# Feed-forward blocks: the input's two transposed halves and the sum of squares in one group of transposes, with the ring of banks used in another order

## The chip, the cores and the metric

The kernel runs on one core of one Trainium2 chip. The metric is the device time of one execution in microseconds (us). Three runs of the kernel before gave 552.25, 552.31 and 552.56 us.

## The reference

The input x has 8 sequences of 1024 tokens with 256 channels. First comes a linear attention with 16 heads (softmax over the head's columns for q, over the tokens for k, a 16 x 16 state for each head), a layer norm, an output projection, the residual and a layer norm. Then comes the feed-forward part, which is what the change touches:

```python
h = layer_norm(x, ln1_g, ln1_b)
h = jnp.einsum('bsd,hd->bsh', h, ternary_quant(w1)) + b1
h = jax.nn.gelu(h, approximate=False)
h = layer_norm(h, ln2_g, ln2_b)
out = jnp.einsum('bsh,dh->bsd', h, ternary_quant(w2)) + b2
...
x = _layernorm(x + _L0_ffn_ref(x, ...), axis=-1)
```

The hidden width is 1024; w1 and w2 are rounded to three values. Everything is float32.

## The kernel before, in words

Every engine has its own hand-written order of work, and semaphores tie the orders together. The attention of the eight sequences fills roughly the first half of the time. The feed-forward part follows, in 16 blocks k of 512 tokens (TB = 4 tiles of 128), and its first three blocks are interleaved with the end of the attention. The names below are the functions of the code; F, S and T are short forms used in this text.

For one block k:

- `ff_norm_apply` (VectorE) scales the four token tiles. `ff_transposes(k, c)` (TensorE, L1945; **T0** and **T1** for c = 0, 1) transposes one half of the channels of the four tiles into one bank, with four 128 x 128 transposes. `ff_ht_high(k, c)` (ScalarE, L854) writes the high part of the bank, `ff_ht_low(k, c)` (VectorE, L1359) the rest.
- `ff_first(k, m)` (TensorE, L2005, **F0** to **F7**) makes 128 of the 1024 hidden columns for 512 tokens with four matmuls. `ff_gelu(k, m)` (ScalarE, L863) works in place in the bank. `ff_square_and_high(k, m)` (ScalarE) writes the square (L879) and the high part (L881). `ff_act_low(k, m)` (VectorE, L1367) writes the rest, `ff_a_lo`.
- `ff_second(k, m)` (TensorE, L2027, **S0** to **S7**) adds both parts times w2 into the four banks of y, with two matmuls for each of four token tiles t. S0 overwrites the banks, and so waits for `ff_centre_y` of the block before, once for each tile t.
- The hidden layer norm is applied after the second product. `ff_hidden_mean` (VectorE, L1391) reads a sum that the second product leaves beside y; `ff_centre_y` (VectorE, L1398, one instruction for each tile) subtracts mean times a row. The squares are summed over the hidden columns on GpSimd (L588) and VectorE (L1378, L1385), and `ff_sum_transposes(k)` (TensorE, L1960) transposes the sum, which `ff_hidden_stats` (VectorE, L1406) reduces.
- `ff_residual`, `ff_out_stats`, `ff_out_shift` (VectorE), `ff_out_rstd` (GpSimd) and `ff_normalise_out` (ScalarE, L896) make the output, `ff_store` (SyncE) writes it.

**The ring.** Banks 0 to 3 are a ring. A block uses 11 places: eight for F, two for T, one for the sum. The place of each use, modulo 4, is its bank (`FIRST_AT`, `HT_AT`, `SUM_AT`), and TensorE waits before each use for what was read last from that bank: `ff_bank_free(k, m)` waits for both the high and the low part of F(k, m). The places follow the order in which TensorE works.

**The order on TensorE** in block k (the loop in the tensor block): T1(k+1), sum(k-1), F3, F4, S0, F5, F6, S1, S2, F7, F0(k+1), S3, F1(k+1), S4, S5, T0(k+2), F2(k+1), S6, S7. So four transposes stand between S5 and F2, and eight between S7 and F3.

**The order on ScalarE** around it: square and high of m = 0 and 1, high part of T0, gelu, square and high of m = 2, two tiles of the output's normalisation, high part of T1, two tiles more, gelu of m = 3 and 4. **On VectorE**: low parts of m = 0 and 1, low part of T0, hidden mean, low part of m = 2, centring of tiles 0 to 3, low part of T1, hidden statistics.

In blocks 1 and 2 ScalarE still has work of the attention between these: `squares` (L812) and `normalise` (L820), four instructions each.

Of the kernel before, what the change touches and what calls it, by code (L numbers as in the profile page):

```python
# [58 lines left out]
def both_halves(nc, x_tok, x_first, x_chan, wq, wk, wv, wo, w1, w2, vecs_d, rows_d, ident_d, mask_d, x1_scratch, out):  # L59
# [3 lines left out]
    CH = C // P  # L63
# [15 lines left out]
    FIRST_AT = (9, 10, 12, 15, 16, 17, 18, 19)  # L79
    HT_AT = (0, 2)  # L80
# [10 lines left out]
    with ExitStack() as ctx:  # L91
# [604 lines left out]
        def _(act):  # L696
# [118 lines left out]
            def normalise(b, g):  # L815
# [3 lines left out]
                for t in range(g * GROUP, (g + 1) * GROUP):  # L819
# [237 lines left out]
            ff_ht_high(2, 0)  # L1057
            ff_gelu(1, 2)
            ff_square_and_high(1, 2)
            squares(NB - 1, 1)  # L1060
            ff_ht_high(2, 1)
# [15 lines left out]
            ff_ht_high(3, 0)  # L1077
            ff_gelu(2, 2)
            ff_square_and_high(2, 2)
            normalise(NB - 2, 0)  # L1080
            ff_ht_high(3, 1)
            ff_gelu(2, 3)
            ff_gelu(2, 4)
            for k in range(3, NK):
# [12 lines left out]
                ff_ht_high(k + 1, 0)  # L1097
                ff_gelu(k, 2)
                ff_square_and_high(k, 2)
                ff_normalise_out(k - 3, (0, 1))  # L1100
# [38 lines left out]
        def _(dve):  # L1139
# [507 lines left out]
            ff_act_low(1, 1)  # L1647
            ff_ht_low(2, 0)
            ff_hidden_mean(0)
            ff_act_low(1, 2)  # L1650
            ff_centre_y(0, (0, 1))
            ff_centre_y(0, (2, 3))
            ff_ht_low(2, 1)
            ff_hidden_stats(0)
            for k in range(1, NK - 1):
# [17 lines left out]
                ff_act_low(k + 1, 1)  # L1673
                ff_ht_low(k + 2, 0)
                ff_hidden_mean(k)
                ff_act_low(k + 1, 2)
                ff_centre_y(k, (0, 1))
                ff_centre_y(k, (2, 3))
                ff_ht_low(k + 2, 1)
                ff_hidden_stats(k)  # L1680
# [31 lines left out]
        def _(pe):  # L1712
# [215 lines left out]
            def ff_transposes(k, c):  # L1928
# [3 lines left out]
                if k == 0 and c == 0:  # L1932
                    pe.wait_ge(et_lo_ok, PAIRS * (NB - 1) + 1)
                if k == 0 and c == 1:
                    pe.wait_ge(et_lo_ok, PAIRS * (NB - 1) + 3)
                if k == 1 and c == 0:
                    pe.wait_ge(et_lo_ok, PAIRS * (NB - 1) + 4)
                if c == 0:
                    if k >= 2:
                        ff_bank_free(k - 2, 6)  # L1940
# [23 lines left out]
            def ff_first(k, m):  # L1964
# [12 lines left out]
                elif m == 2:  # L1977
                    if k < 1:
                        pe.wait_ge(ff_ht_lo_ok, CH * k + 1)
                    else:  # L1980
                        ff_bank_free(k - 1, 7)
                elif m == 3:
                    if k < NK - 1:
                        pe.wait_ge(ff_ht_lo_ok, CH * (k + 1) + 1)
                    else:
                        ff_bank_free(k - 1, 6)
                elif m == 4:
                    ff_bank_free(k, 2)
# [12 lines left out]
                if k == 0 and m == 0:  # L2001
                    pe.wait_ge(et_lo_ok, PAIRS * (NB - 1) + 2)
# [146 lines left out]
            ff_transposes(2, 0)  # L2149
# [82 lines left out]
```

## Time and profile before

| | us |
|---|---|
| median of 3 runs | 552.31 (552.25 to 552.56) |
| the profiled execution | 551.79 |
| its span, first to last instruction | 549.9 |
| TensorE matmul busy | 532.1 (97%) |
| VectorE busy | 481.8 (88%) |
| ScalarE busy | 478.6 (87%) |
| GpSimd busy | 414.7 (75%) |

A busy time is the union of an engine's instructions. Matmuls are pipelined: one matmul's recorded time overlaps the next, and what a matmul costs is the distance from its start to the next one's start (its pitch). The same holds for ScalarE and VectorE, where an instruction's recorded end lies up to 0.1 us behind the start of the next. The idle time in square brackets is that of the engine before the row, with what ended it.

### The profile page before, as it was taken

What the parts mean: (1) busy time and instruction counts of PE and PEld (TensorE: products, weight loads), DVE (VectorE), ACT (ScalarE), POOL (GpSimd) and SP (SyncE); (2) the same over time, 40 slices, a digit from 0 to 9 for tenths busy, and PEclk for the clock granted to TensorE, in tenths of its full rate; (3) what the DMA queues carried; (4) which work ended last, traced back from release to release, by engine and by line L of the source; (5) the groups of instructions that cost most, each with busy time, mean ns of one, the idle gap of its engine ahead of it and who ended that gap; (6) DMA issues with size and microseconds to landing.
All of it is one profiled execution on the core that took longest, in us unless ns stands there. A gap on an engine that the chain in (4) does not pass through costs nothing.

```text
span 549.9 us, 10913 instructions
## 1 busy us (share of the span) xinstructions
PE 532.1 (97%) x3541; PEld 492.0 (89%) x3541; DVE 481.8 (88%) x1227; ACT 478.6 (87%) x952; POOL 414.7 (75%) x429
## 2 busy tenths in 40 slices
PE   8999999999999999989999999999999999999993
PEld 7999999898999989879987999999999999999992
DVE  5888998989899898878788899999999999999896
ACT  5745789798978878778799999999999999999996
POOL 2965969877796986478468878888888877776782
PEclk9999999999999999999999999999999999999997
DMA  8530050320705021070011003322125253010012
GB/s 337 203 122 1 1 230 2 131 100 11 297 1 229 2 87 69 1 266 5 0 40 41 1 0 117 117 76 79 50 68 116 78 93 94 34 53 38 39 40 114
DMA packets 12679, 46.51 MB, mean 85 GB/s; under 512 B 1360, under 2 KB 3792, under 8 KB 10448
## 3 DMA queue, kind: packets, MB, share of 16 engines
q1 hardware_dynamic: 12336, 45.28, 23.7%
q8 instruction: 29, 0.48, 0.4%
q10 hardware_dynamic: 288, 0.54, 0.3%
q14 instruction: 26, 0.21, 0.1%
HBM read 29.01 MB, written 16.81 MB: 83 GB/s over the span
## 4 chain that ended last, share of the span: by engine, by line
PE 68%; ACT 11%; DVE 11%; POOL 5%; issue 3%; DMA 2%; SPq 0%; POOLq 0%; DVEq 0%; ACTq 0%
PE ring L2005 19%; PE qps_sps_aps_then_y L2027 19%; PE qps_sps_aps_then_y L1787 5%; PE qps_sps_aps_then_y L1893 5%; PE qps_sps_aps_then_y L1873 5%; PE ring L1815 5%; DVE z L1285 3%; PE ring L1945 2%; POOL xt_lo L462 2%; PE ring L1920 1%; PE ring L1908 1%; PE ring L1960 1%; ACT ek L745 1%; DMA xc<-in_x_first_dram 1%; POOL ff_accp_over_xt_lo L588 1%
## 5 line engine op out<-in xcount | busy, mean ns | idle before, releaser
L2027 PE MATMUL qps_sps_aps_then_y<-ff_w_over_xc_lo,ff_a_lo_over_qw 128*128 128x258 f32 x512 | 126.5, 283 | 0.0
L2027 PE MATMUL qps_sps_aps_then_y<-ff_w_over_xc_lo,ff_a_hi_over_xc_lo 128*128 128x258 f32 x512 | 126.4, 283 | 0.0
L1367 DVE SCALAR_TENSOR_TENSOR ff_a_lo_over_qw<-ring,ff_rho,ff_a_hi_over_xc_lo 128x512 fp32r<-128x512 f32 x128 | 92.8, 743 | 12.5 <-ACT ff_a_hi_over_xc_lo L881 11.4
L2005 PE MATMUL ring<-ff_ht_hi_over_qw,t 128*128 128x512 f32 x256 | 103.7, 405 | 0.1
L2005 PE MATMUL ring<-ff_ht_lo_over_xc_hi,t 128*128 128x512 f32 x256 | 100.5, 393 | 0.0
L2027 PEld LDWEIGHTS qps_sps_aps_then_y<-ff_w_over_xc_lo,ff_a_lo_over_qw 128*128 128x128 f32 x512 | 96.8, 189 | 3.3
L2027 PEld LDWEIGHTS qps_sps_aps_then_y<-ff_w_over_xc_lo,ff_a_hi_over_xc_lo 128*128 128x128 f32 x512 | 96.7, 189 | 3.4
L863 ACT ACTIVATE ring<-ring,bias 128x512 f32<-128x512 f32 x128 | 84.5, 689 | 6.7 <-PE ring L2005 5.5
L588 POOL TENSOR_TENSOR ff_accp_over_xt_lo<-ff_accp_over_xt_lo,ff_sq_over_ek_et_hi 128x512 f32<-128x512 f32 x66 | 86.0, 1303 | 2.0
L879 ACT ACTIVATE ff_sq_over_ek_et_hi<-ring 128x512 f32<-128x512 f32 x128 | 80.5, 629 | 0.5
L881 ACT CAST ff_a_hi_over_xc_lo<-ring 128x512 fp32r<-128x512 f32 x128 | 79.5, 621 | 0.0
L2005 PEld LDWEIGHTS ring<-ff_ht_hi_over_qw,t 128*128 128x128 f32 x256 | 48.2, 188 | 8.8 <-issue 0.9
L575 POOL TENSOR_TENSOR ff_x1c_over_xt_hi<-ff_x_over_w_raw_xc,ff_c_row 128x512 f32<-128x512 f32 x32 | 37.5, 1192 | 23.9 <-DVE ff_z_over_et_lo L1427 23.9
L2005 PEld LDWEIGHTS ring<-ff_ht_lo_over_xc_hi,t 128*128 128x128 f32 x256 | 48.2, 188 | 7.3
L483 POOL TENSOR_TENSOR qw<-qw,qinv 128x1024 f32<-128x1024 f32 x16 | 31.1, 1942 | 22.2 <-DVE qinv L1186 22.0
L1873 PE MATMUL qps_sps_aps_then_y<-r_hi,pt_hi 128*128 128x384 f32 x128 | 44.7, 349 | 0.7 <-DVE r_lo L1144 0.7
L1873 PE MATMUL qps_sps_aps_then_y<-r_lo,pt_hi 128*128 128x384 f32 x128 | 43.2, 337 | 0.0
L1873 PE MATMUL qps_sps_aps_then_y<-r_hi,pt_lo 128*128 128x384 f32 x128 | 43.1, 337 | 0.0
L462 POOL TENSOR_TENSOR xt_lo<-xt,xt_hi 128x1024 fp32r<-128x1024 f32 x16 | 38.5, 2407 | 2.0 <-ACT xt_hi L728 0.8
L1296 DVE BATCH_NORM_STATS2 bnA<-qps_sps_aps_then_y 128x6 f32<-128x256 f32 x64 | 27.3, 426 | 14.1 <-PE qps_sps_aps_then_y L1873 14.0
L1893 PE MATMUL qps_sps_aps_then_y<-et_hi,xt_hi 128*128 128x256 f32 x128 | 37.4, 292 | 1.9 <-ACT z L776 1.8
L473 POOL TENSOR_TENSOR xt<-xt,c_row 128x1024 f32<-128x1024 f32 x16 | 38.6, 2414 | 0.7
(200 smaller groups left out, 1615.4 us busy)
## 6 DMA issues: line engine op xcount, KB each, us to landing
xt<-in_x_tok_dram SPq DMA_DIRECT2D x8, 1024.0 KB, 4.8
out_dram<-ff_z_over_et_lo SPq DMA_DIRECT2D x15, 512.0 KB, 2.7
x_scratch<-z SPq DMA_DIRECT2D x14, 514.0 KB, 3.6
ff_x_over_w_raw_xc<-x_scratch SPq DMA_DIRECT2D x14, 514.0 KB, 5.1
xc<-in_x_chan_dram SPq DMA_DIRECT2D x6, 1024.0 KB, 6.9
w_raw<-in_w_dram SPq DMA_DIRECT2D x2, 1024.0 KB, 5.4
ek<-in_x_chan_dram SPq DMA_DIRECT2D x1, 1024.0 KB, 8.2
x_scratch<-xt SPq DMA_DIRECT2D x2, 512.0 KB, 7.9
```

What stands on the lines that cost most here:

```text
L462: nc.gpsimd.tensor_tensor(xt_lo[:, ts], xt[:, b % 2, ts], xt_hi[:, ts].bitcast(F32), ALU.subtract).then_inc(xt_lo_ok, 1)
L473: nc.gpsimd.tensor_tensor(xt[:, b % 2, ts], xt[:, b % 2, ts], c_row[:].rearrange("p (o c) -> p o c", o=1).to_broadcast([P, GROUP, C]), ALU ...
L575: nc.gpsimd.tensor_tensor(ff_x1c[:, k % 2, ts], ff_x1[:, k % XB, ts, 0:C], ff_c_row[:].rearrange("p (o c) -> p o c", o=1).to_broadcast([P, ...
L588: nc.gpsimd.tensor_tensor(ff_accp[:], a, ff_sq[:, m], ALU.add).then_inc(ff_sum_p, 1)
L863: nc.scalar.activation(ff_bank(k, m), ff_bank(k, m), ACT.Gelu, bias=bias1[:, m:m + 1]).then_inc(ff_gelu_ok, 1)
L879: nc.scalar.activation(ff_sq[:, m], ff_bank(k, m), ACT.Square).then_inc(ff_sq_ok, 1)
L881: nc.scalar.copy(ff_a_hi[:, m % DEPTH], ff_bank(k, m)).then_inc(ff_hi_ok, 1)
L1367: nc.vector.scalar_tensor_tensor(out=ff_a_lo[:, m % DEPTH], in0=ff_bank(k, m), scalar=ff_rho[:, m:m + 1], in1=ff_a_hi[:, m % DEPTH].bitcas ...
L1873: last = nc.tensor.matmul(out, l, r, start=(c == 0 and k == 0), stop=(c == CH - 1 and k == 2), skip_group_check=True)
L1893: last = nc.tensor.matmul(sps[:, a * C:(a + 1) * C], x, e, start=(t == 0 and a == 0 and k == 0), stop=(t == T - 1 and k == 2), skip_group_ ...
L2005: mm = nc.tensor.matmul(ff_bank(k, m), t1[:, c, m * P:(m + 1) * P], h[:, k % 2, c], start=(c == 0 and j == 0), stop=(c == CH - 1 and j == 1))
L2027: last = nc.tensor.matmul(ff_yps[:, t, 0:C + 2], a[:, m % DEPTH, t * P:(t + 1) * P], ff_w2[:, m], start=(m == 0 and j == 0), stop=(m == FC ...
```

## The change

T0 moves from between S5 and F2 to the place just before T1, so that T0(k+1), T1(k+1) and sum(k-1) stand together, twelve transposes in a row between S7 and F3. The ring's places are changed to this order (`FIRST_AT[2]` from 12 to 11, `HT_AT` from (0, 2) to (1, 2)), and with them the waits: F3 now waits for both parts of F2 of its own block, F4 for the low part of T0, F2 for F6 of the block before. The orders on ScalarE and VectorE are changed to match: on ScalarE one tile of the output's normalisation stands where the high part of T0 stood, and both high parts follow each other; in block 1 `squares` comes after both high parts. On VectorE the low part of m = 2 comes before the hidden mean, and the low parts of T0 and T1 stand between the centring of tile 0 and that of tiles 1 to 3. In block 2 the four `normalise` tiles are split 1, 1 and 2.

```diff
@@ -76,8 +76,8 @@
     TOK = TB * P
     NK = NB * T // TB
     RING = 4
-    FIRST_AT = (9, 10, 12, 15, 16, 17, 18, 19)
-    HT_AT = (0, 2)
+    FIRST_AT = (9, 10, 11, 15, 16, 17, 18, 19)
+    HT_AT = (1, 2)
     SUM_AT = 25
     USES = FC + CH + 1
     DEPTH = 4
@@ -812,11 +812,11 @@
                     nc.scalar.activation(zjunk[:, t % GROUP], z_tile(b, t), ACT.Square, bias=znm[:, t:t + 1],
                                          accum_out=zss[:, t:t + 1]).then_inc(z_sq, 1)
 
-            def normalise(b, g):
+            def normalise(b, g, tiles=range(GROUP)):
                 if not 0 <= b < NB:
                     return
                 act.wait_ge(z_fin, 4 * (NG * b + g + 1))
-                for t in range(g * GROUP, (g + 1) * GROUP):
+                for t in (g * GROUP + n for n in tiles):
                     nc.scalar.activation(z_tile(b, t), z_tile(b, t), ACT.Identity, bias=nmr[:, b % RZ, t:t + 1],
                                          scale=rsZ[:, b % RZ, t:t + 1]).then_inc(x1_ok, 1)
 
@@ -1054,11 +1054,11 @@
             ff_gelu(1, 1)
             ff_square_and_high(1, 0)
             ff_square_and_high(1, 1)
-            ff_ht_high(2, 0)
             ff_gelu(1, 2)
             ff_square_and_high(1, 2)
+            ff_ht_high(2, 0)
+            ff_ht_high(2, 1)
             squares(NB - 1, 1)
-            ff_ht_high(2, 1)
             normalise(NB - 3, 1)
             ff_gelu(1, 3)
             ff_gelu(1, 4)
@@ -1074,11 +1074,13 @@
             ff_gelu(2, 1)
             ff_square_and_high(2, 0)
             ff_square_and_high(2, 1)
-            ff_ht_high(3, 0)
+            normalise(NB - 2, 0, (0,))
             ff_gelu(2, 2)
             ff_square_and_high(2, 2)
-            normalise(NB - 2, 0)
+            normalise(NB - 2, 0, (1,))
+            ff_ht_high(3, 0)
             ff_ht_high(3, 1)
+            normalise(NB - 2, 0, (2, 3))
             ff_gelu(2, 3)
             ff_gelu(2, 4)
             for k in range(3, NK):
@@ -1094,10 +1096,11 @@
                 ff_gelu(k, 1)
                 ff_square_and_high(k, 0)
                 ff_square_and_high(k, 1)
-                ff_ht_high(k + 1, 0)
+                ff_normalise_out(k - 3, (0,))
                 ff_gelu(k, 2)
                 ff_square_and_high(k, 2)
-                ff_normalise_out(k - 3, (0, 1))
+                ff_normalise_out(k - 3, (1,))
+                ff_ht_high(k + 1, 0)
                 ff_ht_high(k + 1, 1)
                 ff_normalise_out(k - 3, (2, 3))
                 ff_gelu(k, 3)
@@ -1645,12 +1648,12 @@
             ff_square_total(0)
             ff_act_low(1, 0)
             ff_act_low(1, 1)
+            ff_act_low(1, 2)
+            ff_hidden_mean(0)
+            ff_centre_y(0, (0,))
             ff_ht_low(2, 0)
-            ff_hidden_mean(0)
-            ff_act_low(1, 2)
-            ff_centre_y(0, (0, 1))
-            ff_centre_y(0, (2, 3))
             ff_ht_low(2, 1)
+            ff_centre_y(0, (1, 2, 3))
             ff_hidden_stats(0)
             for k in range(1, NK - 1):
                 ff_norm_apply(k + 2, (0, 1))
@@ -1671,12 +1674,12 @@
                 ff_residual(k - 1, (2, 3))
                 ff_act_low(k + 1, 0)
                 ff_act_low(k + 1, 1)
+                ff_act_low(k + 1, 2)
+                ff_hidden_mean(k)
+                ff_centre_y(k, (0,))
                 ff_ht_low(k + 2, 0)
-                ff_hidden_mean(k)
-                ff_act_low(k + 1, 2)
-                ff_centre_y(k, (0, 1))
-                ff_centre_y(k, (2, 3))
                 ff_ht_low(k + 2, 1)
+                ff_centre_y(k, (1, 2, 3))
                 ff_hidden_stats(k)
             ff_out_stats(NK - 3, (2, 3))
             ff_act_low(NK - 1, 3)
@@ -1930,14 +1933,14 @@
                     return
                 pe.wait_ge(ff_n_ok, TB * (k + 1))
                 if k == 0 and c == 0:
-                    pe.wait_ge(et_lo_ok, PAIRS * (NB - 1) + 1)
+                    pe.wait_ge(et_lo_ok, PAIRS * (NB - 1) + 2)
                 if k == 0 and c == 1:
                     pe.wait_ge(et_lo_ok, PAIRS * (NB - 1) + 3)
                 if k == 1 and c == 0:
-                    pe.wait_ge(et_lo_ok, PAIRS * (NB - 1) + 4)
+                    pe.wait_ge(et_lo_ok, PAIRS * (NB - 1) + 1)
                 if c == 0:
                     if k >= 2:
-                        ff_bank_free(k - 2, 6)
+                        ff_bank_free(k - 2, 7)
                 else:
                     if k >= 1:
                         ff_bank_free(k - 1, 0)
@@ -1976,16 +1979,16 @@
                         ff_bank_free(k - 1, 5)
                 elif m == 2:
                     if k < 1:
-                        pe.wait_ge(ff_ht_lo_ok, CH * k + 1)
+                        pe.wait_ge(et_lo_ok, PAIRS * NB)
                     else:
-                        ff_bank_free(k - 1, 7)
+                        ff_bank_free(k - 1, 6)
                 elif m == 3:
+                    ff_bank_free(k, 2)
+                elif m == 4:
                     if k < NK - 1:
                         pe.wait_ge(ff_ht_lo_ok, CH * (k + 1) + 1)
                     else:
-                        ff_bank_free(k - 1, 6)
-                elif m == 4:
-                    ff_bank_free(k, 2)
+                        ff_bank_free(k - 1, 7)
                 elif m == 5:
                     if k < NK - 1:
                         pe.wait_ge(ff_ht_lo_ok, CH * (k + 1) + 2)
@@ -1998,8 +2001,6 @@
                         pe.wait_ge(ff_r_sum, k)
                 elif m == 7:
                     ff_bank_free(k, 3)
-                if k == 0 and m == 0:
-                    pe.wait_ge(et_lo_ok, PAIRS * (NB - 1) + 2)
                 for c in range(CH):
                     for j, h in enumerate((ff_ht_hi, ff_ht_lo)):
                         mm = nc.tensor.matmul(ff_bank(k, m), t1[:, c, m * P:(m + 1) * P], h[:, k % 2, c],
@@ -2146,11 +2147,11 @@
             ff_first(1, 1)
             ff_second(0, 4)
             ff_second(0, 5)
-            ff_transposes(2, 0)
             ff_first(1, 2)
             ff_second(0, 6)
             ff_second(0, 7)
             for k in range(1, NK + 1):
+                ff_transposes(k + 1, 0)
                 ff_transposes(k + 1, 1)
                 ff_sum_transposes(k - 1)
                 ff_first(k, 3)
@@ -2166,7 +2167,6 @@
                 ff_first(k + 1, 1)
                 ff_second(k, 4)
                 ff_second(k, 5)
-                ff_transposes(k + 2, 0)
                 ff_first(k + 1, 2)
                 ff_second(k, 6)
                 ff_second(k, 7)
```

## Rows read from the trace of the kernel before

**Rows 1.** The page: busy time and share of TensorE, and its granted clock in 40 slices.

```profile
PE 532.1 (97%) x3541; PEld 492.0 (89%) x3541; DVE 481.8 (88%) x1227; ACT 478.6 (87%) x952; POOL 414.7 (75%) x429
...
PEclk9999999999999999999999999999999999999997
```

**Rows 2.** Twelve blocks: busy PE, PEld, DVE, ACT, POOL, then the granted clock.

```profile
312.97:509.61 196.64, 196.64 (x1298) 180.26 (x1297) 183.20 (x457) 190.73 (x362) 155.77 (x156) 1.00 0.24 71
```

**Rows 3.** Timeline of TensorE around a block's transposes: start us, length us, what.

```profile
391.62 0.60 PE L1945 MATMUL ring<-ident,ff_xn 128*128 128x128 f32 x4
...
392.29 0.39 PE L2005 MATMUL ring<-ff_ht_lo_over_xc_hi,t 128*128 128x512 f32 x1
...
394.91 0.60 PE L1945 MATMUL ring<-ident,ff_xn 128*128 128x128 f32 x4
...
396.01 0.40 PE L2005 MATMUL ring<-ff_ht_lo_over_xc_hi,t 128*128 128x512 f32 x1
...
397.63 0.28 PE L2027 MATMUL qps_sps_aps_then_y<-ff_w_over_xc_lo,ff_a_hi_over_xc_lo 128*128 128x258 f32 x1
...
398.35 0.28 PE L2027 MATMUL qps_sps_aps_then_y<-ff_w_over_xc_lo,ff_a_hi_over_xc_lo 128*128 128x258 f32 x1
```

**Rows 4.** Timeline of ScalarE, the same stretch.

```profile
391.91 0.61 ACT L881 CAST ff_a_hi_over_xc_lo<-ring 128x512 fp32r<-128x512 f32 x1
...
393.19 0.66 ACT L863 ACTIVATE ring<-ring,bias 128x512 f32<-128x512 f32 x1
393.89 0.60 ACT L879 ACTIVATE ff_sq_over_ek_et_hi<-ring 128x512 f32<-128x512 f32 x1
394.38 0.58 ACT L881 CAST ff_a_hi_over_xc_lo<-ring 128x512 fp32r<-128x512 f32 x1
394.85 1.10 ACT L896 ACTIVATE ff_z_over_et_lo<-ff_z_over_et_lo,ff_nmr,ff_rsZ 128x256 f32<-128x256 f32 x2
395.84 0.69 ACT L854 ACTIVATE ff_ht_hi_over_qw<-ring,ff_gain 128x512 fp32r<-128x512 f32 x1
396.41 1.09 ACT L896 ACTIVATE ff_z_over_et_lo<-ff_z_over_et_lo,ff_nmr,ff_rsZ 128x256 f32<-128x256 f32 x2
```

**Rows 5.** Timeline of VectorE, the same stretch.

```profile
395.11 0.17 DVE L1391 TENSOR_REDUCE ff_nmu<-qps_sps_aps_then_y 128x4 f32<-128x8 f32 x1 [0.56 <-PE qps_sps_aps_then_y L2027]
395.31 0.75 DVE L1367 SCALAR_TENSOR_TENSOR ff_a_lo_over_qw<-ring,ff_rho,ff_a_hi_over_xc_lo 128x512 fp32r<-128x512 f32 x1
395.98 1.65 DVE L1398 SCALAR_TENSOR_TENSOR ff_yc_over_xt_lo<-ff_u_row,ff_nmu,qps_sps_aps_then_y 128x256 f32<-128x256 f32 x4
397.54 0.75 DVE L1359 SCALAR_TENSOR_TENSOR ff_ht_lo_over_xc_hi<-ring,ff_gain,ff_ht_hi_over_qw 128x512 fp32r<-128x512 f32 x1
398.20 0.68 DVE L1406 TENSOR_REDUCE ff_sums<-ring 128x4 f32<-128x512 f32 x1
```

**Rows 6.** Timeline of TensorE and VectorE in block 1.

```profile
295.81 0.63 PE L1945 MATMUL ring<-ident,ff_xn 128*128 128x128 f32 x4 [0.94 <-DVE ff_a_lo_over_qw L1367]
...
300.12 0.51 PE L2005 MATMUL ring<-ff_ht_hi_over_qw,t 128*128 128x512 f32 x1
300.46 0.40 PE L2005 MATMUL ring<-ff_ht_lo_over_xc_hi,t 128*128 128x512 f32 x1
...
299.32 0.74 DVE L1359 SCALAR_TENSOR_TENSOR ff_ht_lo_over_xc_hi<-ring,ff_gain,ff_ht_hi_over_qw 128x512 fp32r<-128x512 f32 x1
```

**Rows 7.** Timeline of ScalarE in blocks 1 and 2.

```profile
295.30 0.52 ACT L812 ACTIVATE zjunk<-xt,znm 128x256 f32<-128x256 f32 x1
...
297.28 0.67 ACT L854 ACTIVATE ff_ht_hi_over_qw<-ring,ff_gain 128x512 fp32r<-128x512 f32 x1
...
299.82 1.21 ACT L863 ACTIVATE ring<-ring,bias 128x512 f32<-128x512 f32 x2
...
310.47 0.87 ACT L854 ACTIVATE ff_ht_hi_over_qw<-ring,ff_gain 128x512 fp32r<-128x512 f32 x1
```

**Rows 8.** Waits of TensorE over the whole span: total us, times, longest us.

```profile
PE ring L1960 <- POOL ff_accp_over_xt_lo L588: 0.6, 1, 0.6
```

## The prediction, made before the changed kernel ran

> **What bounds the kernel now.** I read the page first: TensorE is busy for 97% of the span and its granted clock is full in every slice but the last [rows 1]. Then the busy times over twelve whole blocks: TensorE is busy in 196.64 of 196.64 us, so a block takes 16.39 us and TensorE never waits; ScalarE has 190.73 us of work in them and VectorE 183.20 [rows 2], which leaves them 0.49 and 1.12 us a block. The feed-forward part is bound by TensorE's stream, and the change can gain only by taking something out of it, or lose by making it wait. So the rest is a walk along one block, in the timelines of TensorE, ScalarE and VectorE [rows 3 to 5], all in the clock of one block (its T1 at 394.91). The last views are the start-up [rows 6, 7] and the one wait near the end [rows 8].
>
> **The change, part by part.** No instruction is added or removed, and no DMA is moved; SyncE's and GpSimd's orders stay.
>
> *One group instead of two.* T0 alone costs 0.44 us: it starts at 391.62, F2's second matmul at 392.29, less the first matmul's own 0.23 (seven such matmuls lie between 396.01 and S0's start at 397.63) [rows 3]. T1 and the sum together cost 396.01 - 0.23 - 394.91 = 0.87 us [rows 3]. Eight transposes cost twice what four cost, so entering or leaving such a group is free, and a group of twelve will cost 1.31. I take a gain of 0.01 us a block, within the two decimals of the rows. From above it is bound by one transpose, 0.11.
>
> *F2 earlier by 0.44, T0 later.* F2 starts at 391.62, S6 and S7 end 0.44 earlier, T0 starts at 394.47, T1 stays at 394.91, the sum and F3 stay. F2 waits for F6 now, which was read one place earlier than F7: no cost. T0 waits for F7 of two blocks before, long read.
>
> *F3 waits for F2's parts.* ScalarE's new order, with the pitches of rows 4: high part of m = 1 at 391.91; one tile of normalisation at 392.38 (+0.47, as from 394.38 to 394.85); gelu of m = 2 at 392.88 (+0.50, half of 394.85 to 395.84; its bank is ready at 393.19 - 0.44 = 392.75, so ScalarE's queue decides); square +0.70 = 393.58; high part +0.49 = 394.07, which ends 0.58 later, 394.65. ScalarE to VectorE takes 0.03 (gelu's end at 393.85 to the square at 393.89 is of that size) [rows 4]. VectorE is idle by then (it was idle for 0.56 before 395.11 [rows 5]), so the low part of m = 2 runs from 394.68 to 395.43. F3 should start at 396.01 - 0.23 = 395.78: met, with 0.18 to spare after the 0.17 hop found below. No stall.
>
> *The chain behind it.* This is where I expect the loss. From 394.68 VectorE does, by rows 5: low part of m = 2 (0.67, from 395.31 to 395.98), mean (0.20), centring of tile 0 (0.39, a quarter of 395.98 to 397.54), low part of T0 (0.66), low part of T1 (0.66), and centring of tiles 1, 2, 3. These start at 395.35, 395.55, 395.94, 396.60, 397.26, 397.65 and 398.04; the last ends 0.48 later, at 398.52. High parts of T0 and T1 are no limit: T0's bank is ready near 395.1, so they end near 395.8 and 396.4. The hop from VectorE to a waiting matmul is 0.17: in block 1 the low part ends at 299.32 + 0.74 = 300.06, and F5 really runs from 300.46 - 0.23 = 300.23 [rows 6]. So the low part of T0, ended at 396.69, lets F4 go at 396.86 where it was due at 396.71: 0.15 late. S0's fourth tile, due at 398.35 [rows 3], can go at 398.69: 0.34 late, the first stall included. Before, all four tiles were centred by 397.63, when S0 began. Net of the 0.01 it is **0.33 us a block**. It does not heal: gelu of m = 2 hangs on ScalarE's queue, which starts behind F1, and between F1 and S0 TensorE has no slack to shift. It recurs in blocks 3 to 14: 12 x 0.33 = 4.0 us. Bounds: a hop of 0.03 everywhere makes it 0.20 less, so 0.14; were tile 0's transposed low parts slowed as 0.1 us of contention, 0.43. I take 0.33, from rows that show each instruction in this very place.
>
> What hides the rest: the hidden statistics start 0.23 later (398.43 for 398.20), and F6, which waits for them, starts only 1.3 us behind; GpSimd's wait for them grows by as much and it has 3.4 us a block to spare [rows 2].
>
> *Start-up.* In block 1 T1 waits 0.94 us for a low part and is over at 296.44 [rows 6]. Before, `squares` filled this time on ScalarE from 295.30 to 297.28, and the high part of T1 came after [rows 7]. Now the high part comes first and cannot start before 296.48; `squares` follow at 297.05, end 1.98 later, `normalise` takes 1.97 (299.82 - 297.28 - 0.57), and gelu of m = 3 starts at 301.00 instead of 299.82: 1.18 late. From there ScalarE has no idle time up to 310.47 [rows 7], so all of it arrives in block 2: tile of `normalise` at 311.65, gelu 312.15, square 312.85, high part 313.34 to 313.92, and by the same chain (0.03, 3.36 to the last centring, 0.48, 0.17) S0's fourth tile at 317.96. It was due 3.44 behind T1, at 394.91 - 5 x 16.39 + 3.44 = 316.40. So blocks 1 and 2 together lose **1.56 us**. Bounds: 0.6 if ScalarE's delay is caught up, 1.8.
>
> *The end.* Block 15 has no T, only the sum, so F3 stands 0.88 nearer to F2 and waits some 0.7 us. The last sum of squares hides it: TensorE waits 0.6 us there for GpSimd [rows 8], whose additions do not hang on these matmuls closely. I count 0 to 0.2, and take 0.
>
> **Sum.** 4.0 + 1.56 = 5.5 us on the profiled execution's 551.79, so 557.3. That execution is 0.52 below the median of the runs, so I expect **557.8 us**.
>
> *A rule weighed against the rows.* The hops are 0.03 from engine to engine and 0.17 to a matmul in rows 4 and 6. The Trainium skill, Advanced Engine Details and Errata, section Miscellaneous Facts, has 50 to 100 ns for a sequencer's read of a semaphore. With 0.1 at both ScalarE hops the block would lose 0.14 more, some 2 us in all; the rows decide, and they say 0.03.
>
> **The rivals.**
>
> *No wait, same time.* F3's and S0's waits are all met, because VectorE's chain is 0.34 us shorter than I add up. For it: TensorE waits nowhere in twelve blocks now [rows 2], and VectorE has 1.12 us a block free. Against it: the chain starts at ScalarE, not at VectorE's free time, and each length is read in place. It decides at one point: the third centring of the three must end by 398.18. With start-up lag hidden too: 552.2. Chance 0.13.
>
> *The seam was dear.* Each group costs a fixed time beside its transposes, and one is saved. The most the rows leave is 0.11 a block, over 14 blocks 1.5 us: 550.8. Against it: 0.44 and 0.87 [rows 3]. Chance 0.03.
>
> *Only the steady loss.* ScalarE catches up its 1.18 us before block 2: 13 x 0.33 = 4.3, so 556.6. Chance 0.18, slower too.
>
> *The chain is longer.* ScalarE and VectorE slow each other down on the banks, 0.5 us a block: 12 x 0.5 + 1.8, so 560.1. Chance 0.08.
>
> *The clock falls.* Twelve transposes in a row lower TensorE's granted clock, and the eight-matmul stretch behind each group runs at 1.2 instead of 2.4 GHz: 14 x 8 x 0.23 = 26 us, so 578. Against it: the clock stays full through groups of four and of eight, behind TensorE's full work [rows 1, 2]. Chance 0.02. The Trainium skill, TensorE: Matmul & The Clock Gate, Part 4, says that transposes do not count as busy for the gate; by that rule a longer group could cost this.
>
> That the group is not one group can be left out: T1 and the sum wait for the parts of m = 0 and 1, which both engines make before those of m = 2, and these are there in time for F3.
>
> **How the numbers follow.** My forecast has 0.56, the two other slower ones near it 0.26, the clock 0.02: slower 0.84. No wait 0.13: same. Seam 0.03, and 0.01 of the case without waits: faster 0.04, same 0.12. Two runs of this kernel can be told apart from 0.2% on, 1.1 us. The range leaves out the cases without a loss (0.16) and the clock: it begins at 553.8, with both bounds low (12 x 0.14 and nothing from start-up would be 554.0), and ends at 560.2, the longer chain.
>
> **What would show it.** In the changed profile: twelve transposes cost 1.31 us; TensorE idle, or a longer pitch, before F4 and inside S0 at its third and fourth tile, released by VectorE L1398; a period near 16.7 us; in block 1 an idle ScalarE before the second L854, and gelu of m = 3 over 1 us later. I am wrong if the period is still 16.39, or if the waits stand at F3.

## The result, and the profile after

| | before | after |
|---|---|---|
| median, us | 552.28 (551.65 to 552.56, 4 runs) | 559.73 (559.60 to 560.07, 4 runs) |
| the profiled execution, its span | 551.79, 549.9 | 559.60, 557.6 |
| ratio | | 1.0136 (95% interval 1.0124 to 1.0148) |

The changed kernel is slower by 7.45 us; 5.5 were forecast. One execution of block0_place, below, took 750.67 us at a mean granted clock of 0.66, and no number here counts it. In the changed kernel lines have moved by 1 (F is L2006, S L2028) or by 3: T is L1948, the sum L1963, the low parts L1370 and L1362, mean L1394, centring L1401. First the page, which answers to [rows 1], and the busy times over eleven whole blocks, which answer to [rows 2] (PE, PEld, DVE, ACT, POOL, then the granted clock).

```profile
PE 538.4 (97%) x3541; PEld 492.4 (88%) x3541; DVE 483.9 (87%) x1227; ACT 481.3 (86%) x952; POOL 414.5 (74%) x429
...
PEclk9999999999999999999999999999999999999998
```

```profile
331.40:515.80 184.40, 184.40 (x1191) 165.35 (x1190) 169.39 (x418) 176.24 (x331) 141.49 (x144) 1.00 0.27 75
```

TensorE is still shown busy without a gap and at the full clock, for the same 3541 matmuls, and yet a block takes 184.40 / 11 = 16.76 us where it took 16.39. The busy share hides the loss. In the block below a matmul that has waited is recorded as 0.39 or 0.50 us long, where 0.28 or 0.39 is normal, and its record still overlaps that of the matmul before, so no gap appears. Only the starts show the wait. One block in the timeline of TensorE, which answers to [rows 3]:

```profile
398.47 1.04 PE L1948 MATMUL ring<-ident,ff_xn 128*128 128x128 f32 x8
399.34 0.60 PE L1963 MATMUL ring<-ident,ff_accd_over_xt_lo 128*128 128x128 f32 x4
399.70 0.48 PE L2006 MATMUL ring<-ff_ht_hi_over_qw,t 128*128 128x512 f32 x1
400.02 0.40 PE L2006 MATMUL ring<-ff_ht_lo_over_xc_hi,t 128*128 128x512 f32 x1
...
400.77 0.50 PE L2006 MATMUL ring<-ff_ht_hi_over_qw,t 128*128 128x512 f32 x1
401.11 0.40 PE L2006 MATMUL ring<-ff_ht_lo_over_xc_hi,t 128*128 128x512 f32 x1
...
401.81 0.28 PE L2028 MATMUL qps_sps_aps_then_y<-ff_w_over_xc_lo,ff_a_hi_over_xc_lo 128*128 128x258 f32 x1
...
402.60 0.39 PE L2028 MATMUL qps_sps_aps_then_y<-ff_w_over_xc_lo,ff_a_hi_over_xc_lo 128*128 128x258 f32 x1
402.82 0.28 PE L2028 MATMUL qps_sps_aps_then_y<-ff_w_over_xc_lo,ff_a_lo_over_qw 128*128 128x258 f32 x1
402.94 0.40 PE L2006 MATMUL ring<-ff_ht_hi_over_qw,t 128*128 128x512 f32 x1
```

The group of twelve costs 400.02 - 0.23 - 398.47 = 1.32 us: nothing is gained at the seam. F3 does not wait (0.32 to its second matmul; the first after transposes starts early in the records and cost the same before). F4's pitch is 0.34 instead of 0.23. In S0 the third tile's two matmuls and the fourth's first have pitches of 0.14, 0.17 and 0.22 where 0.12 is normal. From 401.81 to F5 at 402.94 are 1.13 us, and eight pitches of 0.12 would be 0.96. Now ScalarE, which answers to [rows 4], and VectorE, to [rows 5]:

```profile
396.89 0.69 ACT L863 ACTIVATE ring<-ring,bias 128x512 f32<-128x512 f32 x1
397.61 0.60 ACT L879 ACTIVATE ff_sq_over_ek_et_hi<-ring 128x512 f32<-128x512 f32 x1
398.10 0.58 ACT L881 CAST ff_a_hi_over_xc_lo<-ring 128x512 fp32r<-128x512 f32 x1
398.57 0.61 ACT L896 ACTIVATE ff_z_over_et_lo<-ff_z_over_et_lo,ff_nmr,ff_rsZ 128x256 f32<-128x256 f32 x1
399.11 1.27 ACT L854 ACTIVATE ff_ht_hi_over_qw<-ring,ff_gain 128x512 fp32r<-128x512 f32 x2
```

```profile
398.72 0.75 DVE L1370 SCALAR_TENSOR_TENSOR ff_a_lo_over_qw<-ring,ff_rho,ff_a_hi_over_xc_lo 128x512 fp32r<-128x512 f32 x1 [0.81 <-ACT ff_a_hi_over_xc_lo L881]
399.38 0.15 DVE L1394 TENSOR_REDUCE ff_nmu<-qps_sps_aps_then_y 128x4 f32<-128x8 f32 x1
399.57 0.48 DVE L1401 SCALAR_TENSOR_TENSOR ff_yc_over_xt_lo<-ff_u_row,ff_nmu,qps_sps_aps_then_y 128x256 f32<-128x256 f32 x1
399.97 1.40 DVE L1362 SCALAR_TENSOR_TENSOR ff_ht_lo_over_xc_hi<-ring,ff_gain,ff_ht_hi_over_qw 128x512 fp32r<-128x512 f32 x2
401.29 1.25 DVE L1401 SCALAR_TENSOR_TENSOR ff_yc_over_xt_lo<-ff_u_row,ff_nmu,qps_sps_aps_then_y 128x256 f32<-128x256 f32 x3
```

The chain of the prediction is there link by link: VectorE idles 0.81 us for the high part of m = 2, then low part, mean, centring, two low parts, three centrings, the last of which ends at 402.54. S0's last tile really starts at 402.82 - 0.12 = 402.70. In ten blocks (4 to 13) this hop is 0.16 us each time, and the one from T0's low part to F4 0.16 or 0.17.

**Where the 7.7 us of span go.** The table compares where F0 of a block starts with the kernel before and takes differences, so the attention's own scatter (its first F0 starts 0.35 us earlier to 0.78 later than before, from one kernel to the next) is the first column and no part of the rest. The runs of the next section stand in it as well.

| span compared with before, us | attention | block 0 | blocks 1, 2 | blocks 3 to 14 (per block) | block 15, end | sum |
|---|---|---|---|---|---|---|
| after | -0.05 | 0.91 | 1.63 | 4.51 (0.376) | 0.76 | 7.76 |
| centre_first | 0.35 | 0.90 | 1.42 | 2.33 (0.194) | 0.77 | 5.77 |
| gelu_first | -0.35 | 0.91 | 0.92 | 0.74 (0.061) | 0.59 | 2.80 |
| gelu_first_squares | -0.08 | 0.92 | 0.04 | 0.61 (0.051) | 0.60 | 2.09 |
| own_places | 0.52 | 0.91 | 1.59 | 4.52 (0.377) | 1.13 | 8.67 |
| own_places_2 | 0.53 | 0.89 | 1.60 | 4.44 (0.370) | -0.03 | 7.43 |
| block0_place | 0.07 | -0.15 | 2.10 | 4.43 (0.369) | 0.76 | 7.22 |
| all_terms | 0.49 | -0.14 | 0.53 | 0.69 (0.058) | -0.02 | 1.55 |
| all_terms_total | 0.63 | -0.16 | 0.31 | 0.70 (0.058) | -0.03 | 1.45 |
| before_centre_late | 0.78 | -0.02 | 1.52 | 3.63 (0.302) | 0.02 | 5.93 |
| before_total_late | -0.10 | -0.01 | -0.15 | 0.00 | -0.01 | -0.27 |

Two terms were not in the forecast's sum: F3's waits in block 0 and at the end. Among TensorE's waits over the span:

```profile
PE ring L2006 <- DVE ff_a_lo_over_qw L1370: 1.8, 3, 0.8
...
PE ring L1948 <- DVE ff_a_lo_over_qw L1370: 0.8, 1, 0.8
```

The three waits of the first line are F3's, in blocks 0 (0.83 us), 2 (0.46) and 15 (0.54). The second line is T1's wait in block 1, which was 0.94 before [rows 6]. In block 0, in the timelines of TensorE and VectorE:

```profile
278.43 0.34 PE L1876 MATMUL qps_sps_aps_then_y<-r_lo,pt_hi 128*128 128x384 f32 x1
279.59 0.47 PE L2006 MATMUL ring<-ff_ht_hi_over_qw,t 128*128 128x512 f32 x1 [0.83 <-DVE ff_a_lo_over_qw L1370]
```

```profile
277.71 0.74 DVE L1362 SCALAR_TENSOR_TENSOR ff_ht_lo_over_xc_hi<-ring,ff_gain,ff_ht_hi_over_qw 128x512 fp32r<-128x512 f32 x1
278.37 0.42 DVE L1299 BATCH_NORM_STATS2 bnA<-qps_sps_aps_then_y 128x6 f32<-128x256 f32 x1
278.71 0.74 DVE L1370 SCALAR_TENSOR_TENSOR ff_a_lo_over_qw<-ring,ff_rho,ff_a_hi_over_xc_lo 128x512 fp32r<-128x512 f32 x1
```

F3 of block 0 now waits for the low part of F2, which VectorE makes behind a transposed low part and an attention statistic; it ends at 279.45. Before, F3 did not need it. At the end, F3 of block 15:

```profile
532.56 0.61 PE L1963 MATMUL ring<-ident,ff_accd_over_xt_lo 128*128 128x128 f32 x4
533.70 0.47 PE L2006 MATMUL ring<-ff_ht_hi_over_qw,t 128*128 128x512 f32 x1 [0.54 <-DVE ff_a_lo_over_qw L1370]
```

From the transposes' start to its own are 1.14 us, and in the kernel own_places_2 below, where it does not wait, 0.36. The kernel before's wait for GpSimd [rows 8] is gone, and still all of the delay reaches the last instruction. The timeline of block 1 on ScalarE answers to [rows 7]:

```profile
295.78 0.69 ACT L854 ACTIVATE ff_ht_hi_over_qw<-ring,ff_gain 128x512 fp32r<-128x512 f32 x1
297.23 0.69 ACT L854 ACTIVATE ff_ht_hi_over_qw<-ring,ff_gain 128x512 fp32r<-128x512 f32 x1 [0.77 <-PE ring L1948]
297.82 0.50 ACT L812 ACTIVATE zjunk<-xt,znm 128x256 f32<-128x256 f32 x1
...
301.76 1.21 ACT L863 ACTIVATE ring<-ring,bias 128x512 f32<-128x512 f32 x2
```

ScalarE idles 0.77 us where the squares used to stand, and gelu of m = 3 starts at 301.76 for 299.82.

### The profile page after: what moved, and what is told of

The parts are those of the page before. It is cut to its first block, busy times and chain, and to the rows that moved or that the text cites. A ratio compares the mean times of both kernels' runs of the same rounds, so it can differ in the third digit from the quotient of the medians.

```text
span 557.6 us, 10898 instructions
## 1 busy us (share of the span) xinstructions
PE 538.4 (97%) x3541; PEld 492.4 (88%) x3541; DVE 483.9 (87%) x1227; ACT 481.3 (86%) x952; POOL 414.5 (74%) x429
## 4 chain that ended last, share of the span: by engine, by line
PE 60%; ACT 14%; DVE 12%; POOL 8%; issue 4%; DMA 1%; POOLq 0%; DVEq 0%; ACTq 0%
PE ring L2006 18%; PE qps_sps_aps_then_y L2028 18%; PE qps_sps_aps_then_y L1790 5%; PE qps_sps_aps_then_y L1876 4%; PE qps_sps_aps_then_y L1896 4%; PE ring L1818 4%; DVE z L1288 3%; POOL xt_lo L462 3%; PE ring L1948 2%; POOL xt L473 2%; ACT ff_a_hi_over_xc_lo L881 2%; ACT z L820 1%; ACT ff_sq_over_ek_et_hi L879 1%; POOL xc_lo L452 1%; PE ring L1923 1%
## 5 line engine op out<-in xcount | busy, mean ns | idle before, releaser
L2028 PE MATMUL qps_sps_aps_then_y<-ff_w_over_xc_lo,ff_a_hi_over_xc_lo 128*128 128x258 f32 x512 | 128.7, 286 | 0.0
L2028 PE MATMUL qps_sps_aps_then_y<-ff_w_over_xc_lo,ff_a_lo_over_qw 128*128 128x258 f32 x512 | 127.5, 283 | 0.0
L1370 DVE SCALAR_TENSOR_TENSOR ff_a_lo_over_qw<-ring,ff_rho,ff_a_hi_over_xc_lo 128x512 fp32r<-128x512 f32 x128 | 92.8, 745 | 25.9 <-ACT ff_a_hi_over_xc_lo L881 25.5
L2006 PE MATMUL ring<-ff_ht_hi_over_qw,t 128*128 128x512 f32 x256 | 104.4, 408 | 2.1 <-DVE ff_a_lo_over_qw L1370 1.8
L2028 PEld LDWEIGHTS qps_sps_aps_then_y<-ff_w_over_xc_lo,ff_a_hi_over_xc_lo 128*128 128x128 f32 x512 | 96.6, 189 | 4.9 <-issue 0.2
L2006 PE MATMUL ring<-ff_ht_lo_over_xc_hi,t 128*128 128x512 f32 x256 | 100.8, 394 | 0.0
L2028 PEld LDWEIGHTS qps_sps_aps_then_y<-ff_w_over_xc_lo,ff_a_lo_over_qw 128*128 128x128 f32 x512 | 96.9, 189 | 3.2
L2006 PEld LDWEIGHTS ring<-ff_ht_hi_over_qw,t 128*128 128x128 f32 x256 | 48.3, 189 | 15.5 <-DVE ff_ht_lo_over_xc_hi L1362 4.8
L2006 PEld LDWEIGHTS ring<-ff_ht_lo_over_xc_hi,t 128*128 128x128 f32 x256 | 48.3, 189 | 7.0
```

Of the source, the lines that this page charges most:

```text
L1370: nc.vector.scalar_tensor_tensor(out=ff_a_lo[:, m % DEPTH], in0=ff_bank(k, m), scalar=ff_rho[:, m:m + 1], in1=ff_a_hi[:, m % DEPTH].bitcas ...
L2006: mm = nc.tensor.matmul(ff_bank(k, m), t1[:, c, m * P:(m + 1) * P], h[:, k % 2, c], start=(c == 0 and j == 0), stop=(c == CH - 1 and j == 1))
L2028: last = nc.tensor.matmul(ff_yps[:, t, 0:C + 2], a[:, m % DEPTH, t * P:(t + 1) * P], ff_w2[:, m], start=(m == 0 and j == 0), stop=(m == FC ...
```

## The experiments

The theory: the loss is separate waits, each set by an order that the change wrote down. (a) In blocks 3 to 14 ScalarE's and VectorE's chain is late for F4 and S0; (b) blocks 1 and 2 lose by the squares' place; (c) block 0's and (d) block 15's F3 wait for a neighbour's bank. Rivals: the merged group itself costs (a longer run of transposes slows what follows), or a mended wait only makes way for the next.

**centre_first**: the last centrings before T1's low part, in both places.

```diff
                 ff_ht_low(k + 2, 0)
-                ff_ht_low(k + 2, 1)
                 ff_centre_y(k, (1, 2, 3))
+                ff_ht_low(k + 2, 1)
```

> The changed kernel, with one change on VectorE: the centring of tiles 1 to 3 comes before the low part of T1 again (behind the low part of T0). My theory (VectorE's chain behind F2 reaches S0's tiles too late): the last centring ends 0.66 us earlier and S0's waits go; the wait of 0.17 us before F4 stays; a block takes 16.56 us instead of 16.77, and with 12 such blocks the time is about 557.3 us (559.7 less 2.4). Rival (the loss belongs to the group of twelve transposes itself, or to TensorE's own order): the period stays 16.77 and the time 559.7.

557.53 us (556.83 to 557.82, 4 runs), ratio to the kernel before 1.0102 (1.0087 to 1.0117). The loss per block falls from 0.376 to 0.194 us with the group of twelve unchanged, so a block takes 16.58 us for 16.56 expected: VectorE's order is half of (a).

**gelu_first**: that, and on ScalarE gelu and square of m = 2 no longer stand behind a tile of normalisation; the same in block 2.

```diff
-                ff_normalise_out(k - 3, (0,))
                 ff_gelu(k, 2)
                 ff_square_and_high(k, 2)
-                ff_normalise_out(k - 3, (1,))
+                ff_normalise_out(k - 3, (0,))
                 ff_ht_high(k + 1, 0)
                 ff_ht_high(k + 1, 1)
-                ff_normalise_out(k - 3, (2, 3))
+                ff_normalise_out(k - 3, (1, 2, 3))
```

> As centre_first, and on ScalarE the tile of output normalisation that stood before gelu of m = 2 is moved behind the high part of m = 2. Theory: gelu starts 0.13 us earlier (then F2 itself sets it), the low part of m = 2 as well, and F4's wait falls from 0.17 to about 0.05 us: period 16.44, time about 555.8 us. Rival (VectorE's own work, not ScalarE's queue, sets the chain): as centre_first, 557.3.

555.50 us (554.62 to 555.69, 4 runs), ratio 1.0064 (1.0049 to 1.0079). 0.061 us per block is left. So ScalarE's order is most of the other half of (a), and of the 4.51 us the merged group itself can have caused 0.74 at most.

**before_centre_late**: the kernel *before*, with its two groups, and only VectorE's order made late.

```diff
-                ff_centre_y(k, (0, 1))
-                ff_centre_y(k, (2, 3))
+                ff_centre_y(k, (0,))
                 ff_ht_low(k + 2, 1)
+                ff_centre_y(k, (1, 2, 3))
```

> The kernel before, with one part of the change alone: on VectorE the low part of T1 comes before the centring of tiles 1 to 3. TensorE and ScalarE are untouched, the groups stay 4 and 8. Theory: the last centring ends at 398.48 in the block's clock instead of 397.63 and S0's last tile waits 0.3 us; 14 blocks, 4.2 to 4.6 us: about 556.7 us. Rival (only the merged group, or F3's new wait, costs time): 552.3.

557.10 us (556.68 to 557.70, 4 runs), ratio 1.0097 (1.0082 to 1.0112), with 0.302 us per block. A loss of nearly the same size appears without the merged group. Its S0 in the timelines of TensorE and VectorE:

```profile
401.15 0.28 PE L2027 MATMUL qps_sps_aps_then_y<-ff_w_over_xc_lo,ff_a_hi_over_xc_lo 128*128 128x258 f32 x1
...
402.06 0.38 PE L2027 MATMUL qps_sps_aps_then_y<-ff_w_over_xc_lo,ff_a_hi_over_xc_lo 128*128 128x258 f32 x1
402.29 0.28 PE L2027 MATMUL qps_sps_aps_then_y<-ff_w_over_xc_lo,ff_a_lo_over_qw 128*128 128x258 f32 x1
```

```profile
400.75 1.26 DVE L1398 SCALAR_TENSOR_TENSOR ff_yc_over_xt_lo<-ff_u_row,ff_nmu,qps_sps_aps_then_y 128x256 f32<-128x256 f32 x3
```

The three centrings end at 402.01, and the last tile really starts at 402.29 - 0.12 = 402.17: again 0.16 behind. Unstalled it would be 401.15 + 6 x 0.12 = 401.87.

The whole loss, 5.2 us, is more than the 4.2 to 4.6 expected: blocks 1 and 2 lose 1.52 us here, though ScalarE's `squares` stand where they stood before. In block 2 ScalarE has its four `normalise` ahead of T1's high part in this kernel, and VectorE, with T1's low part now ahead of the centring, sits idle for it:

```profile
316.62 0.75 DVE L1359 SCALAR_TENSOR_TENSOR ff_ht_lo_over_xc_hi<-ring,ff_gain,ff_ht_hi_over_qw 128x512 fp32r<-128x512 f32 x1 [1.09 <-ACT ff_ht_hi_over_qw L854]
```

The changed kernel has both high parts ahead of the last two `normalise`, so this is not its path. But it shows that the 1.6 us of blocks 1 and 2 can come from more than one order.

**gelu_first_squares**: gelu_first, and in block 1 the squares back between the high parts.

```diff
             ff_ht_high(2, 0)
-            ff_ht_high(2, 1)
             squares(NB - 1, 1)
+            ff_ht_high(2, 1)
```

> As gelu_first, and in block 1 ScalarE's four `squares` stand between the high parts of T0 and T1 again, as in the kernel before. Theory: ScalarE no longer idles before T1's high part (0.77 us), gelu of m = 3 in block 1 starts about 0.8 to 1.1 us earlier, and TensorE's delay after block 2 falls by about 0.9 us: about 554.6 us for gelu_first's 555.5. Rival (block 1's delay comes from block 0 alone): no change.

553.96 us (553.85 to 554.52, 4 runs), ratio 1.0042 (1.0028 to 1.0055). Blocks 1 and 2 cost 0.04 instead of 0.92 us. So of their 1.63 us the squares' place is 0.88; centre_first had taken 0.21 and gelu_first 0.50. (b) holds for the larger part. The two ratios differ by 0.0022, or 1.2 us, with intervals of some 0.8 us to either side, so the traces' 0.9 is the better measure.

**own_places**: other ring places for block 15 alone, which has no T, so that F3 waits for F7 of the block before. The waits are changed to match, here and in the next two kernels.

```diff
+    LAST_FIRST_AT = (9, 10, 11, 12, 13, 15, 16, 17)
+    LAST_SUM_AT = 18
...
```

> The changed kernel, with other places of the ring for block 15 alone, which has no T: F3 and F4 use the two places that T would have used, so F3 no longer waits for block 15's F2. Theory: the wait of 0.8 us before the last block's F3 goes and is not taken by anything else; time 559.0 us (0.7 less). Rival (my prediction's: this wait is hidden at the end by GpSimd's sums): no change, 559.7.

560.29 us (559.59 to 560.50, 4 runs), ratio 1.0150 (1.0133 to 1.0167): a miss. F3's wait is gone and a longer one stands at F6, which in this order got F3's bank. Among TensorE's waits (F is L2004):

```profile
PE ring L2004 <- ACT ff_a_hi_over_xc_lo L883: 0.9, 1, 0.9
```

F3 lies only two F and one S ahead of F6. The block's loss at the end is 1.13 for 0.76.

**own_places_2**: so F3 takes the bank of F7, F4 that of its own block's F2, and F5, F6 and F7 those of F0, of the sum and of F3.

```diff
+    LAST_FIRST_AT = (9, 10, 11, 12, 15, 13, 18, 16)
```

> Second try at the last block. The first moved the wait from F3 to F6, which then followed F3 in the same bank. Here F3 takes T0's free place, F4 waits for F2, F5 takes T1's place, F6 the sum's and F7 follows F3. Theory: no wait of TensorE on the ring in block 15; its delay there, 0.78 us in the changed kernel, is 0 up to the last S7, and the end comes 0.7 us earlier against the start of block 15. Rival (my prediction's: GpSimd's last sum hides it): the wait goes, but the end stays where it was.

558.67 us (558.34 to 559.25, 4 runs), ratio 1.0126 (1.0112 to 1.0140). The end costs nothing now (-0.03), and TensorE's wait for GpSimd is back, in the timeline (the sum is L1964) with the size of [rows 8]:

```profile
546.53 0.65 PE L1964 MATMUL ring<-ident,ff_accp_over_xt_lo 128*128 128x128 f32 x4 [0.60 <-POOL ff_accp_over_xt_lo L589]
```

**block0_place**: other places for F3, F6 and F7 of block 0, so that F3 waits for F1 and F6 for F2. F2 of block 1 then waits for F7 of block 0 and no longer for F6.

```diff
+    ZERO_FIRST_AT = (9, 10, 11, 14, 16, 17, 19, 18)
```

> The changed kernel, with other places for block 0 alone: F3 takes the place of the sum that block 0 does not have, so it waits for F1 and no longer for F2, whose parts come late there. Theory: the delay of 0.95 us at block 0's F3 goes, and about 0.7 to 0.9 us of it is gained at the end: 558.9 us. Rival (the delay is caught up in blocks 1 and 2 by waits for ScalarE and GpSimd anyway): 559.7.

559.05 us (558.38 to 559.50, 3 runs), ratio 1.0130 (1.0111 to 1.0148). Block 0 loses nothing (-0.15 for 0.91), but blocks 1 and 2 lose 2.10 for 1.63, so about half is given back. Some 0.2 us of it is a wait of block 1's F2 for F7's low part, and 0.3 is T1's wait in block 1, which is longer now (T is L1949):

```profile
PE ring L1949 <- DVE ff_a_lo_over_qw L1371: 1.1, 1, 1.1
```

That low part stands behind VectorE's total of block 0's squares (L1389), and this behind GpSimd's additions; TensorE comes to the wait earlier and leaves it not as much earlier.

**before_total_late**: the kernel *before*, with that total moved behind the two low parts, to see how firmly the start-up is held by the other engines.

```diff
-            ff_square_total(0)
             ff_act_low(1, 0)
             ff_act_low(1, 1)
+            ff_square_total(0)
```

> The kernel before, with one edit of its own start-up: VectorE adds GpSimd's sum of squares of block 0 (L1385) after the low parts of block 1's m = 0 and 1 instead of before them. TensorE's wait of 0.94 us before T1 in block 1 falls to about 0. If nothing behind it is bound elsewhere, 551.4 us for 552.3; if ScalarE, which has no idle time from 295 to 311 us, sets the pace of blocks 1 and 2, the gain is under 0.2 us. I expect the second.

551.75 us (551.49 to 552.12, 11 runs) against 551.77 for the kernel before on that chip, ratio 1.0000 (0.9991 to 1.0009). In its trace, counted from F0 of block 0, F3 of block 1 starts 1.3 us earlier and F0 of block 3 only 0.16. The time goes between F7 of block 1 and F5 of block 2, where ScalarE has no gap [rows 7] and most of its instructions start within 0.05 us of where they did.

**all_terms** and **all_terms_total**: all mends together (gelu_first_squares, the places of block0_place and of own_places_2), without and with the total of block 0's squares moved. What the expectations call VectorE's tail of block 15 is these places, and what they call attention's totals is this total.

> The changed kernel with the squares of blocks 1 and 2 put back, ScalarE's and VectorE's order in the group's place changed so that S0 has its halves (as in gelu_first), block 0's third place mended and VectorE's tail of block 15 mended. Theory (the terms are separate and add): 553.96 of gelu_first_squares less 0.7 of the end and less 0.5 to 0.9 of block 0, 552.4 to 552.8, with block 15's F3 and block 0's F3 at their old distances from the block's start and a steady loss of 0.04 to 0.07 us per block left. Rival (something else of the merged group costs, and the terms overlap): 553.4 or more. Nothing in either makes it faster than the kernel before (551.8 to 552.3), since TensorE had no idle time there to give back.

> all_terms, and VectorE's sum of attention's totals (the reduction at L1385 in the kernel before) put behind the low parts of block 1's first two tiles, which in the kernel before brought 1.4 us forward in block 1 and 0.2 from block 2 on. Theory: 0 to 0.3 us below all_terms, 552.1 to 552.7, since ScalarE sets the start of block 2. Rival (with the merged group VectorE sets block 2's start, so the gain stays): 1 us or more below all_terms, which would be faster than the kernel before.

552.94 us (552.40 to 553.35, 11 runs) and 552.88 us (552.60 to 554.21, 11 runs), against 552.22 for the kernel before on that chip: ratios 1.0013 (1.0004 to 1.0022) and 1.0014 (1.0005 to 1.0022). The changed order can be mended to within 0.7 us of the kernel before, and neither beats it. All_terms is 0.72 us above the kernel before; the expectation started from a chip where that kernel took 551.77, and there meant 0.6 to 1.0, so it is met. But the terms do not simply add: blocks 1 and 2 cost 0.53 where gelu_first_squares had 0.04, so here too half of block 0's gain is given back. All_terms_total was expected at up to 552.7; it gains no more than 0.06. Of what is left per block, 0.058 us, more than half stands at one place, in all_terms' timelines of TensorE and VectorE (F is L2011):

```profile
397.82 0.43 PE L2011 MATMUL ring<-ff_ht_hi_over_qw,t 128*128 128x512 f32 x1
398.08 0.39 PE L2011 MATMUL ring<-ff_ht_lo_over_xc_hi,t 128*128 128x512 f32 x1
```

```profile
396.94 0.75 DVE L1362 SCALAR_TENSOR_TENSOR ff_ht_lo_over_xc_hi<-ring,ff_gain,ff_ht_hi_over_qw 128x512 fp32r<-128x512 f32 x1
```

F4's pitch is 0.26 where 0.23 is normal: the low part of T0 ends at 397.69, and with the hop of 0.17 F4 can go at 397.86. T0, high part, low part and F4 now follow each other within one group and F3, where T0 stood 3.3 us ahead before [rows 3]. The other 0.02 to 0.03 are spread over F matmuls, whose pitches are 1 to 3 ns longer on average; why was not tried.

## Why the prediction was right, and where it was not

*The seam.* 1.32 us for twelve transposes against 1.31 forecast: right, and the rival "the seam was dear" falls. The granted clock in whole blocks is 1.00, so the rival of the clock falls too. By the Trainium skill's remark on transposes (TensorE: Matmul & The Clock Gate, Part 4), a longer group could have cost something here; no slice of this trace shows it.

*F3 is met in blocks 3 to 14, F4 and S0 are not.* Right, link by link. Taking 4.00 off (398.47 for 394.467 as the group's start), the low part of m = 2 starts at 394.72 for 394.68, the last centring ends at 398.54 for 398.52, F4 goes at 396.88 for 396.86, S0's fourth tile at 398.70 for 398.69. centre_first, gelu_first and before_centre_late show that these chains are the cause.

*The number.* 559.73 lies inside the range of 553.8 to 560.2, but near its upper end, and nearer to the rival with the longer chain (560.1) than to the forecast of 557.8. That rival's mechanism is not what happened: no point of the chain comes more than 0.04 us later than added up. The time came near it because two terms stood at nothing. The lower bound of the steady loss was also worked out wrongly: with a hop of 0.03 for 0.17 the loss is 0.14 less, which leaves 0.20 a block and not 0.14.

*0.33 us a block* was mis-sized: 0.376 measured, so 4.51 for 4.0. F5 is late by 0.35 instead of 0.33, and the rest comes right after it: the eight matmuls of F5 and F6 have pitches of 0.231 to 0.235 us (medians over ten blocks of the trace), and of 0.226 to 0.232 before. Together that is 0.03 more.

*Blocks 1 and 2, 1.56 us.* 1.63 measured. Gelu of m = 3 is 1.94 late, of which T1 brings 0.76, and the other 1.18 is what was forecast for the squares. By gelu_first_squares their place is 0.88 of the 1.63; the rest is the same order of ScalarE and VectorE as in the steady blocks, which the forecast's chain for block 2 contains. But the agreement is partly luck: with block 0's own loss out of the way they lose 2.10 (block0_place), because TensorE then waits at F2 and longer at T1. The two terms overlap, and I had left the first out. And the loss in block 2 is met first at F3, where I had looked for no wait: by my own times the high part of m = 2 ends at 313.92, the low part at 314.70, and F3 was due at 313.83. So the sign "the waits stand at F3" did come, in blocks 0, 2 and 15, though not in blocks 3 to 14.

*Block 0, not in the sum.* The prediction's step "F3 waits for F2's parts" was worked out only for the steady blocks, where VectorE idles before the low part. In block 0 VectorE has attention statistics there, and the wait costs 0.91 us. Mended (block0_place), blocks 0 to 2 together lose 1.95 instead of 2.54, so its net cost is 0.6.

*The end, counted as 0.* The wait was forecast (some 0.7; 1.14 - 0.36 = 0.78 measured), and the step that failed is "The last sum of squares hides it". The sum is not late: GpSimd's last addition ends 20.89 us behind F0 of block 15, and 21.04 before. But the end does not hang on it. The last residual overwrites the buffer of block 13, and so waits for the store of that block. In the timeline of the kernel before:

```profile
541.71 0.88 DVE L1457 SCALAR_TENSOR_TENSOR ff_z_over_et_lo<-qps_sps_aps_then_y,ff_rsH,ff_x1c_over_xt_hi 128x256 f32<-128x256 f32 x2 [0.32 <-DMA out_dram<-ff_z_over_et_lo]
```

The store waits for four tiles of normalisation on ScalarE, and these stand behind gelu, square and high part of block 15's F7. First ScalarE's timeline of the changed kernel, then its chain of work that ended last:

```profile
541.49 0.66 ACT L863 ACTIVATE ring<-ring,bias 128x512 f32<-128x512 f32 x1
```

```profile
544.78 1.99 ACT ff_z_over_et_lo L896 x4
546.78 2.60 DMA out_dram<-ff_z_over_et_lo
```

From the start of F7's gelu to the last residual are 7.98 us in both kernels and 7.97 to 7.99 in the ten others, and 8.15 or 8.16 more to the last instruction. So what makes F7 late makes the end late in full. The path of the sum and the mean is done 0.32 us ahead of the last residual in the kernel before and 0.13 ahead in the changed one. It too has lost slack, since behind F7's low part VectorE has four statistics before the mean, and GpSimd waits for them:

```profile
545.05 1.39 DVE L1439 BATCH_NORM_STATS2 ff_bnZ<-ff_z_over_et_lo 128x6 f32<-128x256 f32 x4
...
546.94 0.20 POOL L560 TENSOR_TENSOR ff_veZ<-ff_mvZ,eps 128x4 f32<-128x4 f32 x1 [1.05 <-DVE ff_mvZ L1447]
```

That the term is real, 0.8 us, own_places_2 shows. The path through the store is read from the traces and the code; no run moved the store.

*The hops.* The 0.03 to 0.04 from engine to engine and 0.16 to 0.17 to a waiting matmul held wherever they were read: 398.68 to 398.72 on ScalarE to VectorE, 402.54 to 402.70 to S0, 397.69 to 397.86 in all_terms. The block lost 0.04 more than forecast. With the upper end of the Trainium skill's 50 to 100 ns (Advanced Engine Details and Errata, Miscellaneous Facts) at both ScalarE hops it would have lost 0.14 more, and with the lower end 0.04, so the total alone does not speak against the lower end. The rows do: the hop itself is 0.03 to 0.04.

The sum by terms: 0.91 + 1.63 + 4.51 + 0.76 less 0.05 is 7.76 us of span, where 0 + 1.56 + 4.0 + 0 stood.

## What to carry over

In a kernel whose bound engine never idles, moving an instruction gains nothing unless it shortens that engine's own stream; what it surely does is move due times of the other engines, so list for each waiting step the end of what it needs plus the hop, and compare with its due time to 0.05 us. Do this again for the first and the last iterations, where other work stands in the queues: here they were 3.3 of the 7.8 us. At the end of a program, follow the chain that ended last before counting on a wait to hide a delay. And look at starts, not at busy shares, since a pipelined engine can lose 0.38 us in each block and be shown busy all the time.

## What the hardware showed that was not expected

The eight matmuls behind the stall in S0 stay a little longer than before, 0.03 us in all, with the granted clock unchanged. In before_centre_late, which has this stall too, it is 0.02, and in centre_first, which has not, under 0.01; the cause is open. As forecast, the cost of a group of transposes is linear: 0.44, 0.88 and 1.32 us for four, eight and twelve, with a pitch of 0.109 in each. And a late tile shows in two places: in before_centre_late S0's fourth tile is late by 0.18 in its first matmul's recorded start and F5 by 0.28 (medians of ten blocks), since the recorded start of a waiting matmul lies before the point at which it really runs.
